# Where the causal mask of the query-major scores is added: on TensorE as an identity product, or on VectorE in PSUM

## What is computed

```
q, k = rope(unit_norm(q)), rope(unit_norm(k))      # every second head is rotated, head size 32
logits = einsum('bshd,bthd->bhst', q, k) * q_gain
logits = where(causal, logits, most negative)
y = softmax(logits) @ v
x = x + y @ w_out
```

## Time and profile before

| | |
|---|---|
| median of three runs | 2918.4 us (2918.3 to 2919.75) |
| the profiled execution | 2919.15 us, span 2917.4 us |
| PE busy | 2790.7 us, 96% |
| DVE busy | 1770.7 us, 61% |
| ACT busy | 1229.1 us, 42% |
| POOL busy | 414.0 us, 14% |
| granted TensorE clock, mean | 0.991 |
| chain that ended last | PE 85%, DVE 10%, ACT 3% |

### The profile page before, as it was taken

How to read it: one execution, slowest core, us unless ns; L and a number is a source line. 1 busy time by engine, 2 the same in 40 slices (tenths; PEclk the granted TensorE clock), 3 DMA queues, 4 the chain that set the end, 5 groups by cost and what they waited for, 6 DMA issues and landing times.

```text
span 2917.4 us, 56575 instructions
## 1 busy us (share of the span) xinstructions
PE 2790.7 (96%) x23744; PEld 2056.7 (70%) x23744; DVE 1770.7 (61%) x4156; ACT 1229.1 (42%) x2218; POOL 414.0 (14%) x438
## 2 busy tenths in 40 slices
PE   4699989999999999999999999999999999999899
PEld 4467766777777776777767777677777777676576
DVE  8655766556556565665655666565656656566643
ACT  5233553444433444344434445344443444445522
POOL 0103112111030201203011030201103020122000
PEclk8899999999999999999999999999999999999999
DMA  6000000000000000000000000000000000000000
GB/s 247 15 1 1 2 1 1 16 1 16 1 1 16 16 1 1 1 16 16 1 1 1 16 16 1 1 16 9 8 1 1 16 16 1 1 1 8 1 9 15
DMA packets 15485, 37.30 MB, mean 13 GB/s; under 512 B 1408, under 2 KB 1408, under 8 KB 14720
## 3 DMA queue, kind: packets, MB, share of 16 engines
q1 hardware_dynamic: 15232, 33.70, 3.2%
HBM read 25.31 MB, written 8.39 MB: 12 GB/s over the span
## 4 chain that ended last, share of the span: by engine, by line
PE 85%; DVE 10%; ACT 3%; issue 2%; POOL 0%; DMA 0%; SPq 0%; DVEq 0%; ACTq 0%
PE psum L894 24%; PE psum L896 24%; PE psum L895 24%; PE psum L1043 2%; PE psum L1020 2%; PE psum L1056 1%; DVE mneg L808 1%; PE psum L1002 1%; PE psum L937 1%; PE psum L998 1%; PE psum L1044 1%; DVE arena L756 1%; DVE arena L829 1%; PE psum L1021 1%; DVE arena L751 1%
## 5 line engine op out<-in xcount | busy, mean ns | idle before, releaser
L894 PE MATMUL psum<-arena,WG 128*128 128x256 f16 x2048 | 559.0, 273 | 1.4 <-DVE arena L751 1.4
L896 PE MATMUL psum<-arena,WG 128*128 128x256 f16 x2048 | 559.1, 273 | 0.0
L895 PE MATMUL psum<-arena,WG 128*128 128x256 f16 x2048 | 559.0, 273 | 0.0
L894 PE MATMUL psum<-arena,WU 128*128 128x256 f16 x2048 | 558.3, 273 | 0.0
L896 PE MATMUL psum<-arena,WU 128*128 128x256 f16 x2048 | 558.3, 273 | 0.0
L895 PE MATMUL psum<-arena,WU 128*128 128x256 f16 x2048 | 558.2, 273 | 0.0
L756 DVE SCALAR_TENSOR_TENSOR arena<-arena,psum 128x256 f32<-128x256 f32 x512 | 215.0, 420 | 543.4 <-ACT arena L631 542.5
L631 ACT ACTIVATE arena<-psum,tscale 128x256 f32<-128x256 f32 x512 | 242.1, 473 | 662.5 <-PE psum L896 662.3
L894 PE MATMUL psum<-WD,arena 128*128 128x512 f16 x1024 | 388.5, 379 | 12.7 <-DVE arena L762 12.7
L896 PE MATMUL psum<-WD,arena 128*128 128x512 f16 x1024 | 388.5, 379 | 0.0
L895 PE MATMUL psum<-WD,arena 128*128 128x512 f16 x1024 | 388.4, 379 | 0.0
(11 more groups left out here) (142 smaller groups left out, 4662.8 us busy)
## 6 DMA issues: line engine op xcount, KB each, us to landing
arena<-in_L_attn_x SPq DMA_DIRECT2D x16, 512.0 KB, 3.8
out<-arena SPq DMA_DIRECT2D x16, 512.0 KB, 2.8
arena<-in_L_ffn_w_gate SPq DMA_DIRECT2D x4, 1024.0 KB, 9.5
arena<-in_L_ffn_w_up SPq DMA_DIRECT2D x4, 1024.0 KB, 8.8
WD<-in_L_ffn_w_down SPq DMA_DIRECT2D x4, 1024.0 KB, 10.9
arena<-in_L_attn_w_qkv SPq DMA_DIRECT2D x1, 3072.0 KB, 19.5
WQ<-in_L_attn_w_out SPq DMA_DIRECT2D x1, 1024.0 KB, 21.7
ropet<-rope_table SPq DMA_DIRECT2D x1, 128.0 KB, 2.2
```

Source lines behind the costliest of these rows:

```text
L894: T_.matmul(o, lhs(0), rhs(0), start=first, stop=False)
L895: T_.matmul(o, lhs(0), rhs(1), start=False, stop=False)
L896: return T_.matmul(o, lhs(1), rhs(0), start=False, stop=last)
```

## The change

The first pass's product no longer has a mask product behind it. DVE instead adds `maskq` to the diagonal blocks of a bank in PSUM, in place, one instruction for the tiles of a bank (in bank 1 the two blocks are neighbours), and waits for it before it reduces the tiles. Each head gets one more `fill(w)`, behind its last row maximum. The second pass is as before.

```diff
@@ order(), maxima @@
             for bank in range(3):
                 fill(w, False)
                 put(("row max", b, hf, h, bank))
+            fill(w)
@@ block.vector @@
             def row_max(b, hf, h, bank):
                 wait("s1_ps", 3 * head_no(b, hf, h) + bank + 1)
+                n, first = len(QBANKS[bank]), QSEG[QBANKS[bank][0]] + QBANKS[bank][0] * P
+                diagonal = ps(0, first, n * P).rearrange("p (a n) -> p a n", a=n)
+                chained(V_.tensor_tensor(diagonal, diagonal, maskq[:, :].unsqueeze(1).broadcast_to([P, n, P]), ALU.add))
                 for t in QBANKS[bank]:
                     ins = V_.tensor_reduce(mnegv[:, t, h:h + 1], ps(0, QSEG[t], (t + 1) * P), AX_X, ALU.max, negate=True)
                 ins.then_inc(s["smax_done"], 1)
@@ block.tensor, scores_max @@
                         w = (t + 1) * P
-                        T_.matmul(ps(0, QSEG[t], w), QT[0:ST, h, t * P:(t + 1) * P], KT[0:ST, h, 0:w], start=True, stop=False)
-                        ins = T_.matmul(ps(0, QSEG[t] + t * P, P), identb[:, :], maskq[:, :], start=False, stop=True)
+                        ins = T_.matmul(ps(0, QSEG[t], w), QT[0:ST, h, t * P:(t + 1) * P], KT[0:ST, h, 0:w], start=True, stop=True)
```

## The result

The changed kernel took **2948.1 us** (median of 4 runs, 2944.5 to 2948.5) against 2918.9 us before: ratio 1.0097, 95% interval 1.008 to 1.0115. It is slower, as forecast, but by 29 us where 12.9 were forecast, and just outside the stated range of 2906 to 2944.

The account below looks back on a forecast made before the run. TensorE was taken as the bound, fully busy in inner batches but waiting for row maxima in the first and last. Terms: -29.0 + 17.4 + 16.5 + 8.0 = +12.9 us, giving 2931 us (forecast 2925 to 2938, range 2906 to 2944).

Parts of the forecast that it names:

- TensorE's saving: 512 identity products leave TensorE, 0.23 us a head over 128 heads: -29.0 us.
- The price on DVE: Three chained additions a head cost 0.32 + 0.45 + 0.32 = 1.09 us, 140 us over 128 heads.
- rival 4: Chained wait is free: an addition holds DVE only 0.21 or 0.34 us, giving 2912 us; chance 0.08.
- Inner first groups: TensorE waits newly for DVE's maxima, 0.8 us in first halves, 2.1 in second; six inner batches: +17.4 us.
- Rival 1: DVE's lag in the inner batches' first groups is absorbed: 2914 us, or 2906 in its further form; chance 0.25.
- Rival 2: Gating falls behind additions, down products wait in the inner batches' 12 second groups: +13 us, 2944; chance 0.18.
- Outer first groups: First and last batch: DVE alone sets the four stretches' time, 52.4 against 38.2 us; term +16.5 us.
- Outer second groups: First and last batch: 3.6 us saving given back, 1.09 us for each half's last head (4.4): +8.0 us.
- The rest: Outside the first and last batch's first groups, one more piece standing in those groups saves 1.3 us.
- rival 3: Clock falls to half in the four DVE-bound stretches of the first and last batch: +8 us, 2939; chance 0.04.

Follow-up runs that it names:

- c2_fill_no_mask: Kernel before with the added fill, no identity products and no additions, so maxima are taken over unmasked scores: 2898.9 us, 0.9928.
- a3_no_mask: Kernel before without the 512 identity products and with nothing in their place, row maxima over unmasked scores: 2896.4 us, 0.9924.
- c1_outer_first_groups: Changed kernel, but in the first and last batch additions only in first groups; second groups mask by identity products: 2934.8 us, 1.0052.
- a4: Changed kernel with additions and added fill in the six inner batches only; first and last batch as before: 2910.5 us, 0.9967.
- c3: a4 with 0.55 instead of 0.4 beats of filling in the inner batches' first groups: 2900.1 us, 0.9932.
- d1: c3 with 0.7 instead of 0.55 beats of filling in the inner batches' first groups: 2914.2 us, 0.9981.
- a1_fill_only: Kernel before with the added fill alone, masks staying on TensorE: 2923.7 us, 1.0013.
- a2_no_fill: Changed kernel without the added fill: 2977.1 us, 1.0192.
- d2_outer_denser: Changed kernel, additions in all batches, with filling of 0.55 in the inner first groups and 0.8 in the outer ones: 2940.9 us, 1.0076.
- c4_busy_pe: Changed kernel with idle products added in the first and last batch where TensorE waits: 2948.8 us, 1.0099.

## Why the prediction was right or wrong

*TensorE's saving* (-29.0): right. The first two heads of the first group of batch 3 start 3.39 us apart in the kernel before and 3.15 us apart in the changed one, with the same pieces between them: 0.24 us a head where the prediction had 0.23. Without masks the inner batches gain 19 of 22 us.

*The price on DVE* (1.09 us a head): right to 0.02 us, the chained wait included; from start to start the additions take 0.32, 0.46 and 0.32 us (medians). One of 128 columns starts at 309.27 and its reduction at 309.60, 0.33 us for 0.29. By the rule of the Trainium skill ("VectorE: DVE Perf Modes", section "The DRAIN you can't avoid") the wait would have cost nothing; for chained instructions of this size the trace does not agree, and rival 4 is out: none of the 384 is followed before its end.

*Inner first groups* (0.8 and 2.1 us more a batch): right. In batch 3 TensorE's scores wait twice in the first half's group, 0.39 and 0.35 us, and four times in the second half's, 0.64, 0.44, 0.74 and 0.44, beyond the regular distance; 0.7 and 2.3 us. Against the same order without masks (`c2_fill_no_mask`) the two groups are 0.8 and 2.3 us longer. (The prediction's 0.3 us of waiting in the second half today is 0.4 by its own 13.12 - 12.7.) The inner batches still came out 4.8 us better than forecast, since the added fill took away a wait of 0.8 us that the kernel before has at the transposes of each second half's second group, and 0.2 of the waits ahead of the first group. Rival 1 was not it: the waits are there. Rival 2, gating that falls behind, is not seen: the down products wait 12.7 us for the low part of h in both kernels.

*Outer first groups* (13.6, 12.8, 13.2, 12.8 us): right, 13.7, 13.7, 13.5 and 13.0. The second, 0.9 us off, begins in a fall of the clock.

*Outer second groups* (+4.4 us of time, from "1.09 us for the last head of each half"): **the step that failed.** They took 16.9 us more, from 125.0 to 141.9. The corners of the experiments split this: -1.9 for the identity products gone (`a3_no_mask`), +4.3 for the added fill, which puts 66 pieces there instead of 63 (`c2_fill_no_mask` less a3), and **+14.5 for the additions** (the changed kernel less c2). Moving only these additions back to TensorE, identity products included, gave 10.7 us in these stretches and 13 in the whole. The prediction said that this cover was thin and then charged one head in four. It had treated a second group as a queue beside which pieces lie. It is a loop through three PSUM banks, in which query-major scores, maxima, key-major scores and exponentials take turns, and at 6.2 to 7.8 us a head in the kernel before it left little slack. In the four groups TensorE's key-major scores wait 20 times for the maxima in the changed kernel, 7.0 us in all, where they wait 0.3 us in c2, and the transposes at their ends wait 5.7 us against 1.8. Spread over the 16 heads the 14.5 us are 0.9 us a head, most of the 1.09.

*The rest* (forecast -1.3, measured +5.7): also wrong, and of several causes. 1.3 us lie ahead of the first group, where six runs with the same order differ by 2.4 us (286.9 to 289.3), so they mean nothing. Moved pieces give +2.7 us in the projections between the halves of batch 0 (64.5 us against 61.8, and 64.5 with the fill alone too), -1.2 us at the same place of batch 7 and some 1.6 us behind the last group (176.2 us in `c1_outer_first_groups`, 174.6 before, no fall of the clock there in either). Some 3.5 us have the mark of **rival 3**, which had 0.04: the granted clock fell six times for 3.4 us, at 404, 452, 462, 2609, 2626 and 2779 us, while between its start and its end the kernel before shows no fall. In the stretch from the last group of batch 0 to batch 1 two of them cost 3.2 us, which moved pieces outweigh by 2.1. Stretches from the changed kernel (length, then busy us of PE, PEld, DVE, ACT and POOL, then the granted clock): the first group of batch 0, three falls, and a first group of an inner batch:

```profile
288.20:301.90 13.70, 8.80 (x55) 4.46 (x53) 12.68 (x35) 1.36 (x3) 0.00 (x0) 1.00 0.01 1
403.70:407.10 3.40, 3.21 (x15) 2.06 (x16) 2.53 (x8) 0.00 (x0) 0.00 (x0) 0.50 0.00 0
451.50:454.90 3.40, 3.40 (x19) 2.33 (x18) 0.95 (x1) 1.06 (x2) 0.00 (x0) 0.50 0.00 0
461.80:465.20 3.40, 3.40 (x31) 2.40 (x29) 2.30 (x5) 2.65 (x5) 0.00 (x0) 0.50 0.01 2
1391.50:1408.30 16.80, 15.20 (x112) 10.30 (x110) 15.91 (x43) 3.59 (x8) 0.56 (x1) 1.00 0.00 0
```

Summed over the six falls, the distances between starts are some 10 us longer than at 2.4 GHz. That is an upper bound of their cost, since a fall may cost less where DVE sets the pace or a wait follows. Two, at 452 and 462 us, lie where TensorE is busy throughout, and cost 3.2 us. The one at 2779 us costs 0.3: the stretch behind the last group takes 176.4 us with it and 176.2 in `c1_outer_first_groups`, which has the same order and no fall there. The cleanest price comes from two other kernels, which have the same order in batch 7 and the same wait of 2.27 us ahead of this place. In a4 the clock falls behind the wait, in c3 it doesn't:

```profile
2690.30:2693.70 3.40, 3.40 (x26) 2.79 (x24) 1.44 (x3) 1.32 (x2) 0.00 (x0) 0.51 0.02 5
```

From the transposes ahead of it to the next first group a4 takes 63.7 us, c3 62.1: one fall costs 1.7 us where TensorE is busy. Rival 3 had placed the falls wrongly: in the DVE-bound group of batch 0, with TensorE busy for 8.80 of 13.70 us, the clock is 1.00. Only the fall at 404 us, and the last 0.5 us of the one at 2609, lie in a first group. The six begin behind waits of 2.0 to 2.5 us: in the projections, at the transposes that end a group, or at a product with V. The Trainium skill's warning ("TensorE: Matmul & The Clock Gate", section "A second HAM failure mode: psum-queue depth-cycling") agrees with these rows so far as the falls lie among short waits. That such waits bring a fall each time is not shown: a4 and c3 have the same wait, and only one of them falls.

Added up, the forecast's +12.9 became +29.1 by +1.5 in the outer first groups, +12.5 in the outer second groups, +7.0 in the rest and -4.8 in the inner batches. With the second groups alone mis-sized, the time would have come out at the upper end of the range; the rest carried it 4 us beyond, and the unforecast gain in the inner batches hid a part of both. The upper end held rival 2 or the forecast's spread, but no longer loop at every head of the outer batches.

## What to carry to other kernels

Work moved off the busiest engine is worth its full time only in stretches where that engine never waits; read the gain and the price stretch by stretch, not from shares. Where stages of several engines take turns on the same few buffers, count them as a loop: where it has no slack left, what is added to one of its steps is paid at nearly every turn. Work placed beside it fills the waits but does not shorten the turn. A change that gains in most of a program and loses in a part can be limited to where it gains: here additions on DVE in six of eight batches, with more filling beside the first halves' maxima, turned +1.0% into -0.7%.

## What the runs showed of the hardware that was not expected

The granted clock fell to 1.2 GHz for 3.4 us at a time (twice as long in a few runs), in parts of the first and last batch with waits of 0.3 to 2.5 us each between stretches of work. The profiled executions of the kernel before, c3 and d1 have no such fall, that of a4 one (2690 us), of `a3_no_mask` two, of `a1_fill_only` (394, 445 and 2752 us) and `a2_no_fill` three, of `c1_outer_first_groups` and `d2_outer_denser` four, of `c2_fill_no_mask` and `c4_busy_pe` five, of the changed kernel six. `c2_fill_no_mask` has neither products nor additions for the mask, so the additions are not what brings the falls. A fall of 3.4 us cost 0.3 to 1.7 us where it could be priced. Where they come changes with small shifts of the order, so a few us of such a kernel's time hang on it. Adding products in the waits removed two falls and brought another.
